# A vision block on one core: v projected for pairs of images in a padded layout, rotation partners by a VectorE shuffle, scores of the second attention on diagonal tiles

## What is computed

```python
# tok: patches -> rms norm, 8-bit activations, ternary weights -> h (16 images x 37 tokens x 256)
# attention 1, 16 heads of 16:
qkv = x @ Wqkv
re = te * cos - to * sin          # rotation of neighbouring channels of q and k
ro = te * sin + to * cos
num = exp(einsum(q_rot, k_rot) * scale)
den = sum(exp(einsum(q, k) * scale), axis=-1)
attn = where(causal, num / den, 0)
h = h + (attn @ v) @ Wout + bout
# attention 2, 8 heads of 64, each with 8 experts:
gates = sigmoid(x @ w_gate); sel = argmax(gates)
values = einsum(gm, value_experts, x)
attn = softmax(causal(q * scale @ k))
h = h + einsum(gm, output_experts, attn @ values)
```

## Time and profile before

| | |
|---|---|
| median of three runs | 249.35 us (249.26 to 249.85) |
| the profiled execution, its own time | 248.44 us |
| its span, first to last instruction | 246.6 us |
| TensorE busy | 216.5 us (88%), 2047 matmul records |
| VectorE busy | 175.3 us (71%) |
| ScalarE busy | 102.2 us (41%) |
| GpSimd busy | 76.3 us (31%) |
| chain that ended last | PE 60%, DVE 27%, issue 6% of the span |
| mean granted TensorE clock | 0.986 |

### The profile page before, as it was taken

The page is one execution under the profiler, slowest core; times in us unless marked ns, Lnnn a source line. Parts: engine busy times, 40 slices in busy tenths (PEclk is TensorE's granted clock), DMA queues, the critical chain, the costliest instruction groups (busy, mean ns, idle before and its releaser), DMA issues.

```text
span 246.6 us, 5111 instructions
## 1 busy us (share of the span) xinstructions
PE 216.5 (88%) x2047; PEld 190.7 (77%) x2047; DVE 175.3 (71%) x321; ACT 102.2 (41%) x202; POOL 76.3 (31%) x79
## 2 busy tenths in 40 slices
PE   0155879999787899999999999999999999999993
PEld 0035669999674579997768888877989989999993
DVE  1779888654898766942436575666699979979972
ACT  3777859856753216575432161554301111020000
POOL 1152787000342241300506538565934000000000
PEclk9999999999999959999999999999999999999999
DMA  6998000000000020000422005109305154431102
GB/s 177 261 326 352 1 3 1 3 0 0 5 3 3 3 85 1 3 0 0 162 110 85 3 1 185 72 13 254 103 0 169 66 186 142 167 110 49 52 0 100
DMA packets 7181, 20.08 MB, mean 81 GB/s; under 512 B 1043, under 2 KB 1878, under 8 KB 6902
## 3 DMA queue, kind: packets, MB, share of 16 engines
q1 hardware_dynamic: 7158, 19.76, 25.3%
HBM read 19.07 MB, written 0.68 MB: 80 GB/s over the span
## 4 chain that ended last, share of the span: by engine, by line
PE 60%; DVE 27%; issue 6%; ACT 2%; DMA 1%; POOL 1%; DVEq 0%; POOLq 0%
PE ps L263 16%; PE ps L264 15%; PE ps L265 15%; DVE gx L1095 7%; PE ps L1396 3%; DVE rden L927 2%; PE ps L1271 2%; PE ps L1426 2%; DVE oelo L1069 2%; DVE en L910 2%; PE ps L1228 2%; DVE amax L774 1%; DMA xp<-x_rows 1%; DVE stat L803 1%; DVE xhat L814 1%
## 5 line engine op out<-in xcount | busy, mean ns | idle before, releaser
L1033 DVE COPY_PREDICATED v<-onehot,ps 128x512 f32<-128x512 uint8 (+3 forms) x40 | 26.2, 660 | 24.1 <-PE ps L265 23.9
L1095 DVE TENSOR_TENSOR gx<-maskb,oT 128x1184 fp32r<-128x1184 bf16 x31 | 42.3, 1411 | 0.6 <-PE ps L265 0.5
L263 PE MATMUL ps<-gx,oelo 128*128 128x296 f32 x124 | 37.8, 305 | 0.6 <-DVE gx L1095 0.6
L265 PE MATMUL ps<-gx,oehi 128*128 128x296 f32 x124 | 37.2, 300 | 0.0
L264 PE MATMUL ps<-gx,oehi 128*128 128x296 f32 x124 | 37.0, 298 | 0.0
L263 PE MATMUL ps<-vehi,x2lo 128*128 128x512 f32 (+3 forms) x90 | 35.1, 390 | 0.0
L264 PE MATMUL ps<-velo,x2hi 128*128 128x512 f32 (+3 forms) x90 | 33.3, 370 | 0.0
L265 PE MATMUL ps<-vehi,x2hi 128*128 128x512 f32 (+3 forms) x90 | 33.1, 368 | 0.0
L470 POOL TENSOR_TENSOR velo<-veraw,vehi 128x1024 fp32r<-128x1024 f32 x8 | 19.1, 2392 | 23.4 <-ACT vehi L657 18.4
L263 PEld LDWEIGHTS ps<-gx,oelo 128*128 128x128 f32 x124 | 23.3, 188 | 1.8 <-issue 1.3
L264 PEld LDWEIGHTS ps<-gx,oehi 128*128 128x128 f32 x124 | 23.4, 189 | 0.0
(11 more groups left out here) (159 smaller groups left out, 521.9 us busy)
## 6 DMA issues: line engine op xcount, KB each, us to landing
maskb<-mask_rows SPq DMA_DIRECT2D x32, 148.0 KB, 3.6
veraw<-value_w SPq DMA_DIRECT2D x8, 512.0 KB, 3.7
oeraw<-output_w SPq DMA_DIRECT2D x8, 512.0 KB, 3.7
xp<-x_rows SPq DMA_DIRECT2D x6, 336.0 KB, 9.1
wqraw<-w_qkv SPq DMA_DIRECT2D x1, 1280.0 KB, 13.0
w2raw<-w_qkgate SPq DMA_DIRECT2D x1, 1088.0 KB, 15.0
tw<-tok_weight SPq DMA_DIRECT2D x1, 768.0 KB, 7.8
out<-yo SPq DMA_DIRECT2D x4, 148.0 KB, 1.9
```

Source lines behind the costliest of these rows:

```text
L263: pe.matmul(o, llo, rhi, start=start, stop=False)
L265: return pe.matmul(o, lhi, rhi, start=False, stop=stop)
L1033: dve.copy_predicated(v2[0:m, t, h0:h1], bcast(onehot[0:m, t, h0:h1, e], 2, DH2), ps[0:m, JBANK[n], 0:(h1 - h0) * DH2].rearrange("p (a b) ...
L1095: dve.tensor_tensor(gx[:, k % NGR].rearrange("p a b t -> p a (b t)"), bcast(maskb[:, w % NMR, k % MEU], 1, 2), oT[:, c % 2].bitcast(F32), ...
```

## The change

It touches four things.

- **Partners by shuffle.** The swapped weights are gone (`NW` = 3 blocks of weights where 5 were). VectorE makes the partner itself: a stream shuffle of the projection in `ps` into a new tile `partner`, with neighbouring partitions exchanged, as a first step of each rotation. There are 8 qk jobs.
- **v for pairs of images.** x1hi2 and x1lo2 hold every image once, in 64 columns, the last 27 of them zero. A product for two images has 101 stationary columns (`QR` = 64 + 37), so that the second image lands on partition 64. A v job holds four images; there are 4, of 12 matmuls. vblk is set to zero by GpSimd and four reads a job write its blocks.
- **The same padding for keys.** kun, krot, en and ed have 101 rows or columns where 74 were; GpSimd writes zeros in the gaps. The low parts of w2 on GpSimd wait for `en_ready` and `yT_ready`.
- **Later scores on diagonal tiles.** q2 is not masked and doubled; ScalarE writes it with one instruction, not two. Each image and pair of heads has two matmuls of 64 rows by 37 columns, one on rows 0 to 63 with its result on partitions 0 to 36 of bank 2, one on rows 64 to 127 with its result on partitions 64 to 100 of bank 3. `row_max` adds the mask in two instructions, and `sc` is set to zero once.

```diff
         def qk_set(hf, c):
-            return [("qk", hf, c, kind) for kind in range(4)]
+            return [("qk", hf, c, kind) for kind in range(2)]
...
-        PJB = [6, 7, 0, 1] + [2, 3, 4, 5] + [6, 7, 0, 1] + [2, 3, 4, 5] + [6, 7, 0, 1] + [6, 7, 4, 5]
+        PJB = [6, 7] + [0, 1] + [2, 3] + [4, 5] + [6, 7] + [4, 5]
...
-        QSTEPS = 5
+        QSTEPS = 6
...
             pool.memset(half_neg[:], -0.5).then_inc(sm["pool_setup"], 1)
+            for apart in (x1hi2, x1lo2):
+                pool.memset(apart[:, :, :, S:].bitcast(F32), 0.0).then_inc(sm["apart_zero"], 1)
...
+            pool.wait_ge(sm["wqlo_ready"], NW)
+            pool.memset(vblk[:].rearrange("p i h a b -> p (i h a b)"), 0.0).then_inc(sm["vblk_zero"], 1)
+            for keys in (kun, krot):
+                pool.memset(keys[:, :, :, S:DH2], 0.0).then_inc(sm["keys_zero"], 1)
             pool.wait_ge(sm["x1lo_ready"], G)
             for g in range(G):
                 pool.tensor_tensor(h[:, g], h[:, g], biasb[:, 1], ALU.add).then_inc(sm["h0b_ready"], 1)
-            for n in range(4):
-                pool.wait_ge(sm["den_ps"], max(n - 1, 0) + 1)
-                w2_lo(n)
+            pool.wait_ge(sm["en_ready"], 2 * 2)
+            w2_lo(0)
+            pool.wait_ge(sm["en_ready"], 2 * 3)
+            w2_lo(1)
+            pool.wait_ge(sm["yT_ready"], 2)
+            w2_lo(2)
+            w2_lo(3)
...
-                        act.wait_ge(sm["wqlo_ready"], 5)
-                    src = ps[0:2 * S, PJB[n], :].rearrange("p (h a b) -> p h a b", a=2, b=DH1)
-                    dst = vblk[:, 2 * a:2 * a + 2].rearrange("p i h a b -> p (i h) a b")
-                    for p_ in range(2):
-                        ins = act.activation(dst[:, :, p_], src[:, :, p_], ACT.Copy,
-                                             scale=cols("blk2", 2 * S)[:, DH1 * p_:DH1 * p_ + 1])
+                        act.wait_ge(sm["vblk_zero"], 1)
+                    for ii in range(2):
+                        src = ps[DH2 * ii:DH2 * ii + S, PJB[n], :].rearrange("p (i a x) -> p i a x", a=2, x=P)
+                        for p_ in range(2):
+                            dst = vblk[DH2 * p_:DH2 * p_ + S, NVI * a + ii:NVI * (a + 1):2, :, p_]
+                            ins = act.activation(dst, src[:, :, p_].rearrange("p i (h d) -> p i h d", d=DH1), ACT.Copy)
...
-            def x1_pairs(hf):
+            def x1_apart(hf):
...
-                for once, twice in ((x1hi, x1hi2), (x1lo, x1lo2)):
+                for once, apart in ((x1hi, x1hi2), (x1lo, x1lo2)):
                     src = once[:, :, tc].bitcast(F32).rearrange("p c (i s) -> p c i s", s=S)
-                    for p_ in range(2):
-                        act.activation(twice[:, :, im, p_], src, ACT.Copy).then_inc(sm["x1_twice"], 1)
+                    act.activation(apart[:, :, im, 0:S], src, ACT.Copy).then_inc(sm["x1_apart"], 1)
...
-                    own, other = (by_image(ps[:, PJB[m], 0:HALF]) for m in (n, n + 1))
...
-                    dve.wait_ge(sm["proj1_ps"], n + 2)
-                    many(dve.tensor_tensor(part, other, sin, ALU.mult))
                     dve.wait_ge(sm["act_read"], act_reads(n))
-                    step("rope_t", dve.tensor_tensor(tmp, own, cos, ALU.mult))
+                    step("rope_t", dve.stream_shuffle(partner[:, kind], own, [i ^ 1 for i in range(32)]))
+                    many(dve.tensor_tensor(part, by_image(partner[:, kind]), sin, ALU.mult))
+                    step("rope_t", dve.tensor_tensor(tmp, by_image(own), cos, ALU.mult))
                     step("rope_t", dve.tensor_tensor(tmp, tmp, part, ALU.add))
...
-                src = ps[0:2 * S, 2 + g % 2, 0:n * S].rearrange("p (u s) -> p u s", s=S)
-                step("schain", dve.tensor_tensor(sc[:, k, 0:n], src, bcast(cols("cbias", 2 * S), 1, n), ALU.add))
+                for p_ in range(2):
+                    rows = slice(DH2 * p_, DH2 * p_ + S)
+                    src = ps[rows, 2 + p_, 0:n * S].rearrange("p (u s) -> p u s", s=S)
+                    step("schain", dve.tensor_tensor(sc[rows, k, 0:n], src, bcast(cols("cbias")[rows], 1, n), ALU.add))
...
+            step("sc_zero", dve.memset(sc[:].rearrange("p a u s -> p (a u s)"), 0.0))
...
-                else:
-                    pe.wait_ge(sm["sc_ready"], g - 1)
+                if g:
+                    pe.wait_ge(sm["sc_ready"], g)
...
-                        ins = pe.matmul(ps[0:2 * S, 2 + g % 2, u * S:(u + 1) * S], q2[:, c, i].rearrange("p a b -> p (a b)"), k2[:, c, tc],
-                                        start=True, stop=True)
+                        for p_ in range(2):
+                            rows = slice(DH2 * p_, DH2 * (p_ + 1))
+                            ins = pe.matmul(ps[DH2 * p_:DH2 * p_ + S, 2 + p_, u * S:(u + 1) * S], q2[rows, c, tc], k2[rows, c, tc],
+                                            start=True, stop=True)
```

More of the change, by code:

```diff
@@ L45 @@
 C2 = NH2 // 2
+QR = DH2 + S
 OEU = 4
@@ L84, in shape_constants @@
                     + [r // 32 % JS == j for j in range(JS)], 1))
[L85 to L88, removed]
+    k2 = np.arange(S)
+    key = r % DH2
+    put("keep", ((key < S)[:, None] & (key[:, None] <= k2[None, :])).astype(np.float32))
+    put("cbias", np.where((k2[None, :] > (r % DH2)[:, None]) & (r % DH2 < S)[:, None], -BIG, 0.0).astype(np.float32))
+    put("blk2", ((key < S)[:, None] & ((r // DH2)[:, None] == np.arange(32)[None, :] // DH1)).astype(np.float32))
     put("blk", np.concatenate([(t * P + r)[:, None] // S == t * P // S + np.arange(TI_MAX)[None, :]
@@ L171, in vit_block @@
         ropex = sbuf(first, "ropex", [P, 2, HALF])
+        partner = sbuf(first, "partner", [P, 2, HALF])
         qun = sbuf(first, "qun", [P, KC, B, JS, S])
[L173 removed]
+        kun = sbuf(first, "kun", [P, KC, B, QR])
         qrot = sbuf(first, "qrot", [P, KC, B, JS, S])
[L175 to L176 removed]
+        krot = sbuf(first, "krot", [P, KC, B, QR])
+        vblk = sbuf(first, "vblk", [QR, B, PAIRS, 2, DH1])
         w2raw = sbuf(first, "w2raw", [P, KC, W2C])
@@ L203, in vit_block @@
         gateb = sbuf(last, "gateb", [P, C2, T])
[L204 to L209, removed]
+        sc = sbuf(last, "sc", [QR, 2, C2 * GI, S])
+        pe2 = sbuf(last, "pe2", [QR, 2, C2 * GI, S])
+        mx2 = sbuf(last, "mx2", [QR, 2, C2 * GI])
+        sm2 = sbuf(last, "sm2", [QR, 2, C2 * GI])
+        rs2 = sbuf(last, "rs2", [QR, 2, C2 * GI])
+        prob = sbuf(last, "prob", [QR, C2, T])
         ptb = sbuf(last, "ptb", [P, NT, NH2, TI_MAX, S])
@@ L561, in proj_read @@
                 what, a, c, kind = PJ[n]
-                if what == "qk" and kind % 2:
-                    return
                 act.wait_ge(sm["proj1_ps"], n + 1)
@@ L879, in _, with rope @@
             x1_lo(5)
-            def rope(hf, c, kinds=(0, 2)):
+            def rope(hf, c, kinds=(0, 1)):
                 im = slice(hf * B // 2, (hf + 1) * B // 2)
@@ L1166, in proj_job @@
                 pe.wait_ge(sm["x1lo_ready"], GI if n < NEARLY else G)
-                pe.wait_ge(sm["wqlo_ready"], WB[kind] + 1 if what == "qk" else 5)
+                pe.wait_ge(sm["wqlo_ready"], kind + 1 if what == "qk" else NW)
                 if PJPREV[n] >= 0:
@@ L1225, in scores @@
                                 rows = slice(r * P // RT, (r + 1) * P // RT)
-                                key = (kun if kind else krot)[rows, c, i].rearrange("p a b -> p (a b)")
+                                key = (kun if kind else krot)[rows, c, i]
                                 qry = (qun if kind else qrot)[rows, c, i].rearrange("p a b -> p (a b)")
-                                ins = pe.matmul(ps[0:2 * S, 2 * t + r, o:o + JS * S], key, qry, start=True, stop=True)
+                                ins = pe.matmul(ps[0:QR, 2 * t + r, o:o + JS * S], key, qry, start=True, stop=True)
                     ins.then_inc(sm["s_ps"], 1)
```

101 lines of the change are left out of this document (50 added, 51 removed).

## The result

The changed kernel took **260.36 us** (median of four runs, 258.83 to 261.42), the kernel before, beside it, 249.31 (248.55 to 249.85). The ratio is 1.043 (95% interval 1.039 to 1.048). The forecast was 242.5 with 247.3 as upper end. The profiled execution is the one of 258.83 us, its span 256.9.

A forecast was written before the change was run, and what follows sets the result against it. Bounds: TensorE in projections, VectorE's chain in attention 1, TensorE's small products among the values. 2.5 + 2.3 - 0.5 + 2.7 - 0.2 = 6.8 us off 248.44 gives 241.6, plus 0.9 for the median 242.5; range 239.5 to 247.3.

The forecast's parts named there:

- 1.6, and up to 3.5 if it lasts over a block: Cost the clock rival gave for TensorE at 1.2 GHz around the first attend; 244.8 us, chance 0.30.
- the early fall: Rival: TensorE's clock falls earlier, in gaps between 47.9 and 60 us; 244.8, between 244 and 246, chance 0.30.
- VectorE then starts at 37.81 as before.: Projections: VectorE's rotations begin at 37.81 us, waiting for ScalarE's first read, so the eighth kind begins at 58.9.
- 1.25 x 6.9 / 3.8 = 2.3: Projections: 2.3 us of VectorE's rotations lost to GpSimd, scaled from 1.25 us lost in 3.8 us of overlap.
- 2.3 us gained: Attention 1: masks of blocks 1 and 2 fall from 2.53 to 1.38 us each once GpSimd's w2lo moves.
- 0.5 lost: Attention 1: stationary keys of 101 columns for 74 cost 11 ns a score record; 0 as the other end.
- 2.7 gained: Value stage: later scores on small tiles take 5.6 us for 8.4; ends 1.9 lost and 5.3 gained.
- The shuffle: Projections: VectorE's new first step in each rotation, put at 0.55 us with its wait and pattern load.
- a kind at 2.48: Projections: one undisturbed kind of VectorE's rotations, forecast at 2.49 us, 1.94 plus the shuffle's 0.55.
- The projections' 2.5 us: Projections: VectorE's reads that hold back the first attend end at 60.3, not 62.80, so 2.5 us gained.
- the shuffle is dear: Rival, projections: slower than before from 1.4 us a shuffle; 254.0 us at the reciprocal's 1.99; chance 0.06.
- the small tiles don't run side by side: Rival, value stage: later scores take 40 ns a record, 4.6 us more than in the sum, 247.1; chance 0.15.

The follow-up runs named there:

- e15: The changed kernel with GpSimd's memsets behind the last normalisation and its additions on h later, no idle products: 254.89 us median, one execution at 248.0.
- e8: e3 with GpSimd's memsets behind the last normalisation and its additions on h behind the low parts of w2: 244.50 us.
- e1: The changed kernel with GpSimd's large memset of vblk cut into eight pieces, nothing else: 258.67 us.
- e7: The kernel before with each projection product of attention 1 as one matmul instead of three, keys still 74 wide: 242.41 us.
- e3: The changed kernel with both the memset in eight pieces (e1) and the seven idle TensorE products (e2): 244.98 us.
- e2: The changed kernel with seven unread TensorE products: two before each of the last two projection jobs, three before the first attend: 249.38 us.
- e14: The kernel before with only the low parts of w2 on GpSimd moved behind the masks: 247.80 us.
- e13: e9 with scores, exponentials, masks and attention products on 74 rows of keys instead of 101: 240.82 us.
- e9: e8 with three more idle products: before the second and third of the quarter's transposes and the fifth output projection: 242.41 us.
- e4: The kernel before with the later scores on diagonal tiles alone: 247.97 us.
- e10: The changed kernel with scores, exponentials, masks and attention products on 74 of the 101 rows of keys: 248.89 us.
- e5: e3 with only the three idle products before the first attend: 248.45 us, executions in two groups, 244.9 to 245.5 and 248.1 to 249.2.
- e6: e3 with only the four idle products before the last two projection jobs: 255.4 us, scattered from 245.3 to 259.1.
- e11: The kernel before, all projections kept, with 101-column keys (zeros in the gaps) and scores, exponentials and masks on 101 rows: 249.05 us.

## Why the prediction was wrong

The miss is 260.4 - 242.5 = 17.9 us. By medians of kernels that differ in one thing: the changed kernel to e15 is 5.5 (GpSimd's work out of VectorE's way), e15 to e8 is 10.4 (the clock), and e8 still stands 2.0 above the forecast (masks and keys together fell about 1.9 short and the tiles 1.9, against 1.5 from the additions on h that e8 moved; all three below). The first two are not independent at half clock (e1 gave 1.7 for nearly the same freedom), so their split is good to a few us; their sum is 15.9.

**The step that failed most: "1.6, and up to 3.5 if it lasts over a block".** The sum had no term for the clock, and the rival that had one, the early fall, named the right mechanism and the right place, between the last projections and the first attend. Its size was wrong. It let the lower level last a block at most and gave no reason for that; the argument against it was that the kernel before had kept 1.00 at 77% busy. A row at full clock doesn't say how long the lower level lasts once it is there, and the prediction didn't ask what TensorE would do then. The wide scores take 3.00 us a set there and a block 8.15 (attend to attend, 71.78 to 79.93 in the changed kernel's trace), and TensorE is busy without a gap and yet stays at 0.50 until the stage ends. The price is the stage's whole work at half speed: 24.45 us for about 15, so some 10 us where the rival had 3.5 at most. The Trainium skill (TensorE: Matmul & The Clock Gate, What's actually happening) has activity release the lower level. The trace doesn't bear this out for this mix of small float32 products: 24.00 of 24.00 us busy by the profile, granted 0.50; with narrower keys the full clock was back after 4 us in e7. The measurement decides here.

**"VectorE then starts at 37.81 as before."** It started at 41.97 in the profiled run. About 0.9 of that was a late load of the tokens' weights (VectorE waited 1.00 us for it at 10.98, and the last normalisation starts at 35.93 for 34.99 before), the rest the lock. The prediction took GpSimd's disturbance as a share of the overlap (1.25 x 6.9 / 3.8 = 2.3), from the additions on h, and looked for it in the rotations alone. But the memset met the last normalisation, and held it for its own whole length: 3.57 us for 0.41, 0.59 with the memset in pieces (1.51 in e3), 0.41 with it behind. The Trainium skill (SBUF — State Buffer, Who interferes with whom) has this rule, an exclusive lock for a whole instruction; the prediction cited it and applied it only to the masked copies. The changed kernel's trace agrees with it (3.57 us beside a memset of 3.51); in e2 the normalisation was held over three memsets in a row.

**"2.3 us gained" by the masks, and "0.5 lost" by the keys.** The masks became as short as forecast (1.46). But in the kernel before 0.7 of it reaches the first output projection (e14), and with wide keys TensorE becomes the last at 4.67 us a block, which takes 1.6 (e13). The records cost what the sum said (1.65 for 1.29, 0.36 a set); wrong was to charge them only in front of masks and reciprocals while taking the whole of the masks' gain. Attention 1 has two chains of nearly equal length, and shortening one while lengthening the other gave nothing: 15.06 us in e9, 14.94 before.

**"2.7 gained" by the tiles.** The size of the group was right (0.98 in the chain, 1.05 in the timeline, 1.06 forecast). The gain was 0.8 (e4), since the softmax behind the groups comes into the chain.

**Right.** The shuffle (0.50 for 0.55), a kind at 2.48, short masks, the groups of later scores. The estimate by the Trainium skill (VectorE: DVE Perf Modes, the perf-mode tier table), 0.57 for the shuffle, is about as near. The projections' 2.5 us were there too, once VectorE was free: in e3 the first attend starts at 60.46 for 62.87, 2.4 us earlier. e8 and e9, with the additions on h moved as well, start it at 58.97 and 58.74, a gain that the sum didn't have. The rivals "the shuffle is dear" and "the small tiles don't run side by side" fell. The idle products of e9 bring 242.4 us, the forecast's number, but that is chance: e9 also removes a dip that the sum left in. The range's upper end, 247.3, doesn't follow from its words either: by the prediction's own prices the clock alone reached 246.0, the serial tiles alone 247.1 and both together 248.7 at least.

**What stays open.** Why the clock stays low with 101-column keys and doesn't with 74: the runs show that both the light projections and the wide keys are needed, not what the chip counts. The clock was also low before the stage in several runs, 0.69, 0.74 and 0.84 in the changed kernel's three stretches of 4 us from 40 to 52, and 0.50 and 0.53 in e10's two from 40 to 48, and it came back there under the long products of the projections; under the wide scores it didn't. e10's case is unexplained in part, since TensorE does less there before the first attend than in the changed kernel (1.69 us busy of 4 from 60 to 64, for 2.02) and keeps 1.00. Filling ahead of the stage elsewhere than at the two places of e5 and e6 was not tried.

## What to carry to other kernels

When a change takes work off TensorE in front of a stage of small products, price the lower clock over that whole stage, not over one block, and read the granted clock first when the result comes. Idle products in the gap are a cheap test, and here the remedy: seven of them gave 11.0 us, and with the lock removed and three more idle products 260.4 became 242.4. Don't let a long GpSimd memset stand beside a VectorE scaling between two SBUF tiles (3.57 us for 0.41 here); put it behind, or cut it up (0.59 to 1.51). And when an experiment shows no cost, look whether it moved something else that paid for it, as e11's masks did.

## What the runs showed of the hardware

- The granted clock stayed at 0.50 for 24 us while the profile had TensorE busy all the time, and whether a program is caught in it can differ between executions: 245.3 us at a mean clock of 0.986, or 254.8 to 259.1 at 0.92 to 0.94 (e6).
- It can fall before the small products begin (e1, 0.60 from 52 to 56 us).
- One 3.51 us GpSimd memset held a 0.41 us VectorE tensor_scalar for 3.57 us, and three in a row, 5.05 us, held it for 5.12 (e2).
- A VectorE stream shuffle of 128 x 296 float32 from PSUM takes 0.48 to 0.50 us, a product's time (0.46 to 0.47); loading its pattern is 0.01.
- Scores of 37 by 37 on diagonal tiles run at 0.98 / 48 = 20 ns a record; stationary operands of 101 for 74 columns cost 52 for 40 ns.
